# Matmuls without readers in TensorE's pauses: one decoder layer of cross attention and a quantised feed-forward block

## The chip, the cores and the metric

The kernel runs on one core of one Trainium2 chip. Its time is the device time of one execution in microseconds (us); a comparison takes the median of several executions. TensorE (PE) multiplies matrices, VectorE (DVE), ScalarE (ACT) and GpSimd (POOL) do the elementwise work, SyncE (SP) issues nearly all of the transfers. TensorE's clock is granted at one of two levels, 1.2 GHz (0.50 in the profile's rows) and 2.4 GHz (1.00).

## The reference

```python
x = x + cross_attention(layernorm(x), ctx)     # x 16 x 100 x 512, ctx 16 x 361 x 256, fp32
#   q = h @ Wq, k = ctx @ Wk, v = ctx @ Wv; 16 heads of 128; q and k through an RMS norm per head with gains
#   softmax(q k' / sqrt(128)) v, all heads joined, @ Wo
x = x + h_bitlinear(silu(gate) * up, w_down)   # gate, up = h_bitlinear(layernorm(x), w_gate / w_up)
#   h_bitlinear: Walsh-Hadamard rotation of the row, rounding to 8 bits by the row's largest value,
#   product with weights rounded to -1, 0, 1; 512 -> 2048 -> 512
```

## The kernel before

The kernel has three stages, each a block of its own: all engines finish one before any begins the next. An engine runs its instructions in the order written. An fp32 product is built from three fp32r matmuls (high by high, low by high, high by low), whose high and low parts ACT and DVE make.

**Queries** (`queries`). The 1600 tokens go in four groups of four sequences. For a group, DVE normalises the tokens (`xn`), TensorE transposes them into `psX` (`transposes`, L284), ACT and DVE split them into `xT_hi` and `xT_lo`, and for each of the 16 heads TensorE does 12 matmuls of 400 columns into `psQ` (L323), which ACT drains twice (`q_out`, stored to DRAM by SP, and the squares `sq`). `squares` (L295) sums the squares of four heads, DVE adds a constant (`ms`), and `factors` (L304) transposes the sums. Ahead of the first group Wq is fetched in pieces of 1 MB into a staging area of two halves. A piece may land in its half only when the piece before has been split, and ACT splits piece 2 only behind its drains of heads 0 and 1. The order on TensorE is: wait for the identity (`d_id`) and three of POOL's constants (`g_const`), transposes of group 0, the groups, and after the last group `squares` and `factors`.

**Attention** (`attention`). TensorE makes keys for a head (L732, 6 matmuls of 362 columns), and a product for head m waits until DVE has finished `k_lo` of head m - 2. After five heads `squares` (L744) sums the first four heads' squares; DVE, SP, POOL and a transfer turn them into the row factors `rk`, on which the first softmax waits. The later part is a pipeline of 64 units.

**Feed-forward** (`feed_forward`). 13 tiles of 128 tokens. `out_proj(t)` (L1296) is the output projection of tile t, 48 matmuls of 512 columns into `psA`. For tile 0 it stands ahead of the steps; its first half uses weights made in the stage before (`wo_first`), its second half weights that this stage fetches, splits on ACT and DVE, and counts in `v_w`. Then the chain for a tile is: residual and layer norm (DVE, with a power on POOL, L1224), `norm_T` (4 transposes, L1304), the split on ACT and DVE, `rotate_in` (8 matmuls of 256 columns, L1318), the row's scale and rounding, `q1_T` (L1327), `gate_up` (4 blocks of 8 matmuls of 512 columns, L1343), silu on ACT, product and rotation by DVE and POOL, `hidden_T` (transposes, L1355), `rotate_hidden` (L1365), rounding, a transposing transfer `turn_q2` by SP, and `down` (16 matmuls of 512 columns, L1375). `step(i)` holds work of up to four tiles (i to i + 3) in the order written, so that in the middle of the stage one tile's chain is hidden behind another tile's matmuls. Steps -2 and -1 fill this pipeline and steps 11 and 12 (`TILES - 2`, `TILES - 1`) empty it; from step 10 on no output projection is left. `high_o` and DVE's `o_lo` split the tile's input `o_in` (fetched by SP, L1160), and in step -2 DVE does this between the statistics and the norm of tile 0.

Of the kernel before, what the change touches and what calls it, by code (L numbers as in the profile page):

```python
# [22 lines left out]
P = 128  # L23
# [25 lines left out]
TILES = -(-T // TT)  # L49
# [72 lines left out]
def queries(nc, sbt, sem, passed, weights, ident, rq_all, neg_half, asums, d_q, x, wq, wk, wv, gq, gk, w_ff, ctxT,  # L122
# [7 lines left out]
    with ExitStack() as ctx:  # L130
# [25 lines left out]
        g_const, g_rstd, g_rq = s("g1_const"), s("g1_rstd"), s("g1_rq")  # L156
# [84 lines left out]
        @block.gpsimd  # L241
        def _(pool):
            nc.gpsimd.memset(neg_half[:], -0.5).then_inc(g_const, 1)
            nc.gpsimd.memset(sel[:], 0.0).then_inc(g_const, 1)
            pool.wait_ge(g_const, 2)
            nc.gpsimd.memset(sel[:, QW32 - 1:QW32], 1.0).then_inc(g_const, 1)
            nc.gpsimd.memset(weights["ones"][:], 1.0)
            for part in (cT_hi, cT_lo):
                nc.gpsimd.memset(part[:, :, :, SK:SKP].bitcast(F32), 0.0)

            def norm(g):
                pool.wait_ge(v_ve, g + 1)
                nc.gpsimd.tensor_tensor(rstd[:], ve[:], neg_half[0:SQ, :].to_broadcast([SQ, GB]),
                                        op=ALU.pow).then_inc(g_rstd, 1)

            def rms(g, part):
                pool.wait_ge(v_rq, g + 1)
                query_factors(nc, rq_all, neg_half, g, part).then_inc(g_rq, 1)

            def group(g, first, last):  # L260
                for h in range(H):
                    if h == 5 and not last:
                        norm(g + 1)
                    if 6 <= h < 14 and not first:
                        rms(g - 1, h - 6)

            norm(0)
            group(0, True, False)
            with pool.Fori(1, G - 1) as g:
                group(g, False, False)  # L270
            group(G - 1, False, True)

        @block.tensor
        def _(pe):
            pe.wait_ge(d_id, 16)
            pe.wait_ge(g_const, 3)

            def transposes(g):
                if due(g * DC):
                    pe.wait_ge(v_xlo, g * DC)  # L280
                for b in range(GB):
                    pe.wait_ge(v_xn, g * GB + b + 1)
                    for c in range(DC):
                        last = nc.tensor.transpose(psX[c][:, b * SQ:(b + 1) * SQ], xn[:, b, c * P:(c + 1) * P], ident[0:SQ, 0:SQ])  # L284
                    last.then_inc(p_xT, 1)

            def squares(g, k):

                pe.wait_ge(a_q, g * H + k * HG + HG)
                if k == 0:  # L290
                    if due(g):
                        pe.wait_ge(v_ms, g)
                for j in range(HG):
                    rows = slice(j * QW32, (j + 1) * QW32)
                    last = nc.tensor.matmul(psS[rows, 0:GT], sel[:, QW32 - 1 - k:2 * QW32 - 1 - k], sq[:, k % 2, j, :],  # L295
                                            start=(k == 0), stop=(k == NG - 1), tile_position=(0, j * QW32))
                last.then_inc(p_ss, 1)

            def factors(g):
                pe.wait_ge(v_ms, g + 1)  # L300
                pe.wait_ge(v_rq, g)
                apart(pe, pe_passed)
                for b in range(GB):
                    last = nc.tensor.transpose(psR[0:SQ, b, :], ms[:, b * SQ:(b + 1) * SQ], ident[:])  # L304
                last.then_inc(p_rq, 1)

            def group(g, first, last_group):
                for h in range(H):
                    if first and h == 0:
                        pe.wait_ge(v_first, 1)  # L310
                    elif first and h % HG == 0:
                        pe.wait_ge(used[h // HG % 2], h // HG // 2 + 1)
                    if first and h == 2:
                        pe.wait_ge(used[0], 1)
                    if due(g * H + h - 1):
                        pe.wait_ge(a_q, g * H + h - 1)
                    n = 0
                    for c in range(DC):
                        if h == 0:
                            pe.wait_ge(v_xlo, g * DC + c + 1)  # L320
                            apart(pe, pe_passed)
                        for w, m in ((wq_hi, xT_hi), (wq_hi, xT_lo), (wq_lo, xT_hi)):
                            last = nc.tensor.matmul(psQ[h % 2][:, 0:GT], w[:, c, h * D:(h + 1) * D], m[:, c, :],  # L323
                                                    start=(n == 0), stop=(n == 3 * DC - 1))
                            n += 1
                        if h == H - 1 and c < DC - 1:
                            last.then_inc(p_read, 1)
                    last.then_inc(p_q, 1)
                    if h % HG == 1 and h > HG:
                        squares(g, h // HG - 1)  # L330
                    elif h == 1 and not first:
                        squares(g - 1, NG - 1)
                    if h == 4 and not first:
                        factors(g - 1)
                    if h == 10 and not last_group:
                        transposes(g + 1)

            transposes(0)
            group(0, True, False)
            with pe.Fori(1, G - 1) as g:  # L340
                group(g, False, False)
            group(G - 1, False, True)
            squares(G - 1, NG - 1)
            factors(G - 1)

        @block.scalar
# [724 lines left out]
def feed_forward(nc, sbt, sem, passed, ident, neg_half, w127, o_in, d_stored, d_first, x, wo, d_wo, wo_first, had_in, o_dram,  # L1071
# [10 lines left out]
    with ExitStack() as ctx:  # L1082
# [56 lines left out]
        def real(t):  # L1139

            return not isinstance(t, int) or 0 <= t < TILES
# [138 lines left out]
        def _(pe):  # L1280
            def out_proj(t, heads):
                if heads[0] == 0:
                    if not (isinstance(t, int) and t == 0):
                        pe.wait_ge(v_o, NO + 1)
                    if due(t - 1):
                        pe.wait_ge(g_o, t - 1)
                    if due(t):
                        pe.wait_ge(v_xT, t)
                for h in heads:
                    if isinstance(t, int) and t == 0 and h % 2 == 0:  # L1290
                        pe.wait_ge(v_o, h // OH + 1)
                        if h >= HALF:
                            pe.wait_ge(v_w, (h - HALF) // 2 + 1)
                    hi, lo = (a[:, h, :] if h < HALF else b[:, h - HALF, :] for a, b in zip(wo_first, (wo_hi, wo_lo)))
                    for i, (w, m) in enumerate(((o_hi, hi), (o_hi, lo), (o_lo, hi))):
                        last = nc.tensor.matmul(psA[:], w[:, h, :], m, start=(h == 0 and i == 0),  # L1296
                                                stop=(h == H - 1 and i == 2))
                if heads[-1] == H - 1:
                    last.then_inc(p_out, 1)
# [69 lines left out]
            def down(t, k, rotated):  # L1369
# [7 lines left out]
                if k == 1:  # L1377
                    last.then_inc(p_down, 1)

            def step(i):  # L1380
                front = i + 2 if not isinstance(i, int) else min(i + 2, TILES)
                for j in range(NB):
                    if real(i + 1):
                        gate_up(i + 1, j)
                if real(i + 2):
                    out_proj(i + 2, range(AHEAD, H))
                if real(i + 1):
                    hidden_T(i + 1, 0)
                    hidden_T(i + 1, 1)
                if real(i):  # L1390
                    down(i, 0, front)
                    down(i, 1, front)
                if real(i + 1):
                    rotate_hidden(i + 1, 0)
                    hidden_T(i + 1, 2)
                    rotate_hidden(i + 1, 1)
                    hidden_T(i + 1, 3)
                if real(i + 2):
                    norm_T(i + 2)
                if real(i + 1):  # L1400
                    rotate_hidden(i + 1, 2)
                    rotate_hidden(i + 1, 3)
                if real(i + 2):
                    rotate_in(i + 2)
                if real(i + 3):
                    out_proj(i + 3, range(0, 4))
                if real(i + 2):
                    q1_T(i + 2)
                if real(i + 3):
                    out_proj(i + 3, range(4, AHEAD))  # L1410

            pe.wait_ge(v_ident, 1)
            out_proj(0, range(0, AHEAD))
            pipeline(pe, step, 3)
# [311 lines left out]
```

## Time and profile before

| | |
|---|---|
| median of 3 runs | 1480.15 us (1478.39 to 1481.29) |
| the profiled execution's own time | 1479.02 us |
| its span, first to last instruction | 1477.2 us |
| mean granted TensorE clock | 0.985 |
| TensorE busy | 1408.9 us, 95% of the span |
| VectorE, ScalarE, GpSimd busy | 65%, 64%, 35% |
| queries, attention, feed-forward | to 188 us, to 1050 us, to the end |

Busy is the time in which an engine had an instruction under way. A busy TensorE says nothing of its clock: at 1.2 GHz the same matmul is busy for longer. The idle time before an instruction, and what ended it, stand in square brackets at the end of its row.

### The profile page before, as it was taken

Reading aid. Unit: us, or ns where it says so; the run is one execution under the profiler, and the core shown is the slowest. Engines: PE = TensorE matmul, PEld = TensorE weight load, DVE = VectorE, ACT = ScalarE, POOL = GpSimd, SP = SyncE. Lnnn points to the kernel's source line nnn. Section 1 sums busy time; section 2 is a strip of 40 time slices with the busy share of each in tenths; the row PEclk is TensorE's granted clock in tenths of the full one; section 3 lists DMA queues with packets and bytes.
Section 4 is the critical chain, followed back from the end, with each engine's and each line's share of the span. In section 5 each row is a group of like instructions: output and inputs, shape, how many; then the busy total and the mean of one; then the engine's idle time right before and its main releaser. Section 6 shows DMA issues by size and latency. Waiting matters only on the chain. (4 is left out here: it accounts for less than half of the span.)

```text
span 1477.2 us, 30157 instructions
## 1 busy us (share of the span) xinstructions
PE 1408.9 (95%) x8818; PEld 1207.3 (82%) x8818; DVE 953.3 (65%) x2464; ACT 946.8 (64%) x2069; POOL 522.1 (35%) x323
## 2 busy tenths in 40 slices
PE   6999989999999999999999999998789999999995
PEld 6888868999999999999999999998566777677752
DVE  5312056677777777777777777766466777677764
ACT  4556658878888888788888788877324343434431
POOL 0033324433332223322333322335244555455533
PEclk9999999999999999999999999999899999999998
DMA  7767723343444443344434444334623223322211
GB/s 240 215 177 192 206 73 85 103 111 106 119 122 112 120 125 100 109 126 128 106 115 117 113 118 128 100 92 133 202 56 88 57 64 85 78 57 64 64 36 29
DMA packets 187782, 165.05 MB, mean 112 GB/s; under 512 B 111040, under 2 KB 162256, under 8 KB 185872
## 3 DMA queue, kind: packets, MB, share of 16 engines
q1 hardware_dynamic: 180752, 151.21, 37.5%
q10 hardware_dynamic: 6912, 12.59, 2.6%
q8 instruction: 35, 0.57, 0.2%
q14 instruction: 83, 0.68, 0.1%
HBM read 123.44 MB, written 33.14 MB: 106 GB/s over the span
## 5 line engine op out<-in xcount | busy, mean ns | idle before, releaser
L698 POOL TENSOR_TENSOR rk_sp<-ms_sp,neg_half 76x10 f32<-76x10 f32 (+1 forms) x128 | 242.2, 1908 | 596.0 <-DMA ms_sp<-ms 596.0
L1021 DVE CUSTOM_DVE_ANT_0 sc<-psS,rk 100x361 f32<-100x361 f32 x256 | 136.3, 532 | 108.1 <-PE psS L756 82.8
L873 ACT ACTIVATE pr<-ex,ri 100x361 f32<-100x361 f32 x256 | 152.9, 597 | 79.6 <-DVE ri L1010 79.4
L866 ACT ACTIVATE ex<-sc,nb,rq 100x361 f32<-100x361 f32 x256 | 175.2, 685 | 9.7 <-DVE nb L1028 9.5
L732 PE MATMUL psK<-cT_hi,wk_hi 128*128 128x362 f32 x512 | 171.1, 334 | 1.1 <-DVE k_lo L991 1.1
L854 ACT ACTIVATE k_hi<-psK 128x362 fp32r<-128x362 f32 x256 | 120.6, 471 | 78.3 <-PE psK L732 77.4
L732 PE MATMUL psK<-cT_lo,wk_hi 128*128 128x362 f32 x512 | 168.7, 330 | 0.0
L732 PE MATMUL psK<-cT_hi,wk_lo 128*128 128x362 f32 x512 | 168.6, 329 | 0.0
L991 DVE TENSOR_TENSOR k_lo<-psK,k_hi 128x362 fp32r<-128x362 f32 x256 | 134.5, 525 | 8.6 <-ACT sq L860 7.3
L781 PE MATMUL psZ<-pT_hi,cK_hi 120*128 120x400 f32 (+1 forms) x384 | 132.8, 346 | 0.0
L781 PE MATMUL psZ<-pT_hi,cK_lo 120*128 120x400 f32 (+1 forms) x384 | 132.3, 345 | 0.0
L781 PE MATMUL psZ<-pT_lo,cK_hi 120*128 120x400 f32 (+1 forms) x384 | 132.3, 345 | 0.0
L794 PE MATMUL psNV<-z,wv_sb 128*128 128x100 f32 x1024 | 124.9, 275 | 1.4 <-issue 1.4
L794 PEld LDWEIGHTS psNV<-z,wv_sb 128*128 128x128 f32 x1024 | 119.4, 192 | 2.0 <-issue 2.0
L769 PEld LDWEIGHTS psP<-ident,pr 100*120 100x120 f32 (+1 forms) x768 | 79.8, 165 | 48.0 <-issue 27.7
L860 ACT ACTIVATE sq<-psK 128x362 f32<-128x362 f32 x256 | 118.5, 463 | 0.0
L769 PE MATMUL psP<-ident,pr 100*120 100x100 f32 (+1 forms) x768 | 96.9, 262 | 7.1 <-ACT pr L873 6.9
L732 PEld LDWEIGHTS psK<-cT_hi,wk_hi 128*128 128x128 f32 x512 | 97.3, 190 | 5.6 <-DVE k_lo L991 4.4
L1002 DVE TENSOR_TENSOR pT_lo<-psP,pT_hi 121x600 fp32r<-121x600 f32 x128 | 99.0, 774 | 4.2 <-ACT pT_hi L881 3.0
L323 PE MATMUL psQ<-xT_hi,wq_hi 128*128 128x400 f32 x256 | 92.1, 360 | 6.1 <-ACT sq L397 3.0
L732 PEld LDWEIGHTS psK<-cT_lo,wk_hi 128*128 128x128 f32 x512 | 97.8, 191 | 0.0
L732 PEld LDWEIGHTS psK<-cT_hi,wk_lo 128*128 128x128 f32 x512 | 97.3, 190 | 0.0
(169 smaller groups left out, 3416.5 us busy)
## 6 DMA issues: line engine op xcount, KB each, us to landing
rk<-rk_dram SPq DMA_DIRECT2D x64, 564.1 KB
o_in<-o_dram SPq DMA_DIRECT2D x13, 1024.0 KB, 6.0
q_dram<-q_out SPq DMA_DIRECT2D x64, 200.0 KB, 4.4
q_in<-q_dram SPq DMA_DIRECT2D x64, 200.0 KB, 4.9
o_dram<-o SPq DMA_DIRECT2D x64, 200.0 KB, 5.4
stage<-in_w_ff SPq DMA_DIRECT2D x12, 1024.0 KB, 6.3
w_in<-in_w_ff ACTq DMA_DIRECT2D x48, 256.0 KB, 3.0
cT_in<-in_ctxT SPq DMA_DIRECT2D x16, 361.0 KB, 5.1
```

The costliest lines, as they stand in the source:

```text
L698: nc.gpsimd.tensor_tensor(rk_sp[:, cols], ms_sp[:, cols], neg_half[0:HG * SKR, :].to_broadcast([HG * SKR, n]), op=ALU.pow).then_inc(g_rk, 1)
L732: last = nc.tensor.matmul(psK[h % 2][:, 0:SKP], w[:, c, col:col + D], x[:, slot, c, :], start=(n == 0), stop=(n == 3 * CC - 1))
L769: last = nc.tensor.transpose(psP[0:KW[i], k, i * SQ:(i + 1) * SQ], pr[:, 2 * half + k, KO[i]:KO[i] + KW[i]], ident[0:SQ, 0:SQ])
L781: last = nc.tensor.matmul(psZ[c][:, 0:UQ], w[0:KW[i], slot, i, c * P:(c + 1) * P], x[0:KW[i], j % 2, i, :], start=(n == 0), stop=(n == 8))
L794: last = nc.tensor.matmul(psNV[:, h * SQ:(h + 1) * SQ], wv_sb[:, c, col:col + D], z[:, j % 2, c, h * SQ:(h + 1) * SQ], start=(c == 0), sto ...
L854: nc.scalar.activation(k_hi[:, j, h, :], psK[h % 2][:, 0:SKP], ACT.Copy)
L860: nc.scalar.activation(sq[:, j % 2, h, :], psK[h % 2][:, 0:SKP], ACT.Square).then_inc(a_k, 1)
L866: nc.scalar.activation(ex[:, h % 2, :], sc[:, h % 2, :], ACT.Exp, bias=nb[:, h % 2:h % 2 + 1], scale=rq[:, j % 2, h:h + 1], accum_out=rs[: ...
L873: nc.scalar.activation(pr[:, h, :], ex[:, h % 2, :], ACT.Copy, scale=ri[:, h % 2:h % 2 + 1]).then_inc(a_pr, 1)
L991: nc.vector.tensor_tensor(k_lo[:, j, h, :], psK[h % 2][:, 0:SKP], k_hi[:, j, h, :].bitcast(F32), ALU.subtract).then_inc(v_klo, 1)
L1002: nc.vector.tensor_tensor(two_heads(pT_lo, j, half), psP[0:KW[0], :, 0:3 * SQ].rearrange("p k (i q) -> p k i q", q=SQ), two_heads(pT_hi, j ...
L1021: nc.vector.tensor_tensor_reduce(out=sc[:, h % 2, :], in0=psS[0:SQ, 0:SK], in1=rk[:, j % 2, h, :], scale=1.0, scalar=-3.0e38, op0=ALU.mult ...
```

## The change

Two helpers, both called `busy`, issue matmuls with `start=True, stop=True` into a PSUM bank whose content nobody reads before the next real product overwrites it. No engine waits for them, and they wait for nothing of their own but what stands ahead of them on TensorE. The wait for POOL's constants becomes one for a fourth constant (`ones`) and comes ahead of the wait for the identity.

| place | matmuls | columns, type |
|---|---|---|
| ahead of the first transposes | 22 | 128, fp32 |
| after the first transposes | 11 | 128, fp32 |
| after the last head, ahead of `squares` | 4 | 400, fp32r |
| after it, ahead of `factors` | 6 | 400, fp32r |
| ahead of the first output projection | 6 | 512, fp32r |
| step -2, ahead of and after `norm_T(0)` | 27 and 5 | 512, fp32r |
| step 10, ahead of `q1_T(12)` | 11 | 512, fp32r |
| step 11, ahead of `hidden_T(12, 0)` | 27 | 512, fp32r |
| step 12, ahead of `down(12, 0)` | 27 | 512, fp32r |

```diff
-            nc.gpsimd.memset(weights["ones"][:], 1.0)
+            nc.gpsimd.memset(weights["ones"][:], 1.0).then_inc(g_const, 1)
...
+            def busy(bank, w, m, count):
+                for _ in range(count):
+                    nc.tensor.matmul(bank[:, 0:m.shape[-1]], w, m, start=True, stop=True)
+
+            pe.wait_ge(g_const, 4)
+            busy(psQ[0], weights["ones"][:], weights["ones"][:], 22)
             pe.wait_ge(d_id, 16)
-            pe.wait_ge(g_const, 3)
...
             transposes(0)
+            busy(psQ[0], weights["ones"][:], weights["ones"][:], 11)
             group(0, True, False)
...
             group(G - 1, False, True)
+            busy(psX[0], wq_hi[:, 0, 0:P], xT_hi[:, 0, :], 4)
             squares(G - 1, NG - 1)
+            busy(psX[0], wq_hi[:, 0, 0:P], xT_hi[:, 0, :], 6)
             factors(G - 1)
...
+            def busy(bank, count):
+                for _ in range(count):
+                    nc.tensor.matmul(bank[:], wo_first[0][:, 0, 0:P], wo_first[0][:, 0, :], start=True, stop=True)
...
                     out_proj(i + 2, range(AHEAD, H))
+                if isinstance(i, int) and i == TILES - 2:
+                    busy(psA, 27)
                 if real(i + 1):
                     hidden_T(i + 1, 0)
                     hidden_T(i + 1, 1)
+                if isinstance(i, int) and i == TILES - 1:
+                    busy(psA, 27)
                 if real(i):
                     down(i, 0, front)
...
                     hidden_T(i + 1, 3)
+                if isinstance(i, int) and i == -2:
+                    busy(psT[0], 27)
                 if real(i + 2):
                     norm_T(i + 2)
+                if isinstance(i, int) and i == -2:
+                    busy(psT[0], 5)
...
                     out_proj(i + 3, range(0, 4))
+                if isinstance(i, int) and i == TILES - 3:
+                    busy(psA, 11)
                 if real(i + 2):
                     q1_T(i + 2)
...
+            busy(psT[0], 6)
             pe.wait_ge(v_ident, 1)
             out_proj(0, range(0, AHEAD))
```

## Rows read from the trace of the kernel before

**Rows 1.** The page, part 2: granted clock in tenths, 40 slices of 37 us.

```profile
PEclk9999999999999999999999999999899999999998
```

**Rows 2.** Windows: length, busy (instructions) of PE, PEld, DVE, ACT, POOL; granted clock, DMA, GB/s.

```profile
187.40:194.20 6.80, 6.21 (x22) 5.66 (x21) 2.77 (x12) 1.67 (x4) 0.00 (x0) 0.50 0.26 84
...
1051.00:1057.80 6.80, 6.16 (x15) 4.83 (x16) 3.93 (x7) 3.60 (x6) 0.39 (x1) 0.50 0.90 310
...
1068.00:1078.10 10.10, 4.25 (x15) 3.58 (x16) 5.55 (x8) 0.60 (x1) 3.61 (x3) 0.50 0.79 244
...
1429.80:1436.60 6.80, 5.19 (x15) 2.00 (x16) 2.33 (x7) 3.68 (x5) 0.00 (x0) 0.50 0.40 77
```

**Rows 3.** Timeline, PE, feed-forward: start, duration, instruction, idle before it and its releaser.

```profile
1072.44 1.11 PE L1304 MATMUL psA<-ident,xr 128*128 128x128 f32 x4 [6.76 <-DVE xr L1567]
...
1430.63 0.61 PE L1327 MATMUL psT<-ident_b,q 128*128 128x128 bf16 x4 [2.76 <-DVE q L1611]
1432.02 9.48 PE L1343 MATMUL psB<-wt,q1T 128*128 128x512 fp8e4 x32 [0.78 <-ACT q1T L1456]
1448.10 1.97 PE L1355 MATMUL psT<-ident,stage 128*128 128x128 f32 x8 [6.60 <-DVE stage L1655]
...
1467.55 5.20 PE L1375 MATMUL psF<-wt,q2T 128*128 128x512 fp8e4 x16 [6.76 <-issue]
```

**Rows 4.** The chain that ended last, in order of time: start, us, what.

```profile
1051.64 14.05 PE psA L1296 x48
...
1074.97 2.07 PE psF L1318 x8
1077.04 3.38 PE psA L1296 x12
...
1124.30 0.87 PE psT L1355 x8
1125.17 3.45 PE psF L1375 x16
...
1134.04 0.96 PE psF L1318 x8
1135.00 2.76 PE psA L1296 x12
...
1403.23 7.06 PE psB L1343 x32
...
1450.07 5.32 PE psF L1375 x16
```

**Rows 5.** Timeline, PE, ACT and SP, first query group.

```profile
16.54 2.76 SPq L199 DMA_DIRECT2D stage<-in_wq  x2
...
19.51 0.54 PE L323 MATMUL psQ<-xT_lo,wq_hi 128*128 128x400 f32 x1
...
20.34 0.34 PE L323 MATMUL psQ<-xT_lo,wq_hi 128*128 128x400 f32 x1
...
22.32 1.92 ACT L354 ACTIVATE wq_hi<-stage 128x2048 fp32r<-128x2048 f32 x1
```

**Rows 6.** DMA issues, window 16 to 18 us: KB each, us from issue to landing.

```profile
stage<-in_wq SPq DMA_DIRECT2D x1, 1024.0 KB, 5.1
```

**Rows 7.** Timeline, PE, first keys of the attention.

```profile
188.88 0.65 PE L732 MATMUL psK<-cT_hi,wk_hi 128*128 128x362 f32 x1
...
197.24 0.81 PE L744 MATMUL psNV<-sq,sel 128*32 128x362 f32 x8
...
199.15 0.44 PE L732 MATMUL psK<-cT_hi,wk_hi 128*128 128x362 f32 x1
...
201.92 0.43 PE L732 MATMUL psK<-cT_hi,wk_hi 128*128 128x362 f32 x1
```

**Rows 8.** Timeline, SP, first load of `o_in` in the feed-forward.

```profile
1053.59 0.49 SPq L1160 DMA_DIRECT2D o_in<-o_dram  x1
```

**Rows 9.** DMA issues, window 1053.5 to 1054 us.

```profile
o_in<-o_dram SPq DMA_DIRECT2D x1, 1024.0 KB, 10.3
```

## The prediction, written before the changed kernel ran

> **What bounds the kernel now.** I read the page first. TensorE is busy for 95% of the span, so I looked for what it does at the half clock and where it stands still on the path to the end. The clock line of the page [rows 1] is nearly full everywhere and dips in the 29th slice and at the end; a slice is 37 us, so it hides stretches of a few us. Windows cut at the edges show them [rows 2]: the granted clock is 0.50 in 187.4 to 194.2, 1051.0 to 1057.8, 1068.0 to 1078.1 and 1429.8 to 1436.6. The reader is to see there that TensorE is busy for 6.2, 6.2, 4.3 and 5.2 us of these stretches, doing needed work at 1.2 GHz. The timeline and the chain show two more of the kind behind the pauses at the very end (below). In the first queries the clock record stands at full, but the durations tell another thing [rows 5]: the matmul at 19.51 takes 0.54 us and the same form at 20.34 takes 0.34. I take that stretch, from the first matmul at 14.0 to about 19.9, as cold too.
>
> Then the timeline of TensorE [rows 3] for what comes ahead of each cold stretch: pauses of 6.76, 2.76, 6.60 and 6.76 us, each ended by another engine or a transfer. The chain [rows 4] shows that the matmuls behind them are themselves on the path. Between 200 and 1040 us and from 1080 to 1428 us the clock is full, and the change touches nothing there.
>
> So the change is worth what the cold stretches cost on the path, if its matmuls hold the clock, and it costs what they overrun the pauses by.
>
> **What one added matmul costs.** Its form in the feed-forward, 512 columns of fp32r, is that of the output projection: 12 take 2.76 us warm [rows 4], 0.230 each. Cold, the windows row has 15 in 6.16 us [rows 2], 0.41 (0.43 from start to start, by the twofold clock). So 27 take 6.2 us warm against pauses of 6.76, 6.60 and 6.76; 11 take 2.5 against 2.76 [rows 3]. Each block ends 0.2 to 0.6 us before the real work is released, and nothing is queued behind it but that work. The 400-column ones at the end of the queries and the 128-column ones at the start lie ahead of waits too. The fp32 form with 128 columns does not occur before; its nearest relatives are transposes of 128 columns, 0.109 each warm (8 in 0.87) [rows 4], and I allow it from that to 0.43 (a cold 512-column one). 22 are then between 2.4 and 9.4 us behind a start near 1 us: at the upper end they would reach into the first transposes, whose result waits for the first piece of Wq anyway. I take them as hidden. The eleven behind the transposes take 1.2 to 4.7 us, in a pause of about two; I take 0, with up to 2.5 of loss if they run cold.
>
> **Start of the queries.** Warm, the stretch 14.0 to 19.9 would shrink by 0.34/0.54 or more, about 2.8 us. But TensorE is not what follows. ACT splits piece 2 of Wq at 22.32, without a wait, right after its drains of heads 0 and 1 [rows 5]. SP issued that piece at 16.54, when its half of the staging area came free, and it landed 5.1 us later, at 21.64 [rows 6]. Earlier drains leave ACT waiting for it, so the later splits, the next piece's load and the stores queued on SP behind it move by 22.32 - 21.64 = 0.7 us. Gain 0.7 (bounds -2.5 and +2.8).
>
> **End of the queries, start of the attention.** The added 4 and 6 matmuls of 400 columns stand before two waits. The 6.8 us of cold clock end at 194.2 [rows 2]; keys begin at 188.88 and the first `squares`, behind five heads, at 197.24 [rows 7]. Warm, a pair of heads takes 201.92 - 199.15 = 2.77 us, paced by the ACT and DVE work between product m - 2 and m. Five heads then end at 188.88 + 2 x 2.77 + 6 matmuls (6 x 0.18 = 1.1) = 195.5. `squares` starts 1.7 us earlier, and the chain behind it, through a transfer, POOL and a second transfer to the first softmax, moves with it. Gain 1.7 (bounds 0, if the chain is caught by something fixed, and 2.0).
>
> **First output projection.** 48 matmuls take 14.05 us [rows 4] and would take 48 x 0.230 = 11.0 warm, 3.0 less; the second half's weights arrive just in time for that, so 2.8. The six added ones take 1.4 us between the block's start at 1050.0 and the first real one at 1051.64. The stage boundary ahead of them stays idle. What is late next is `o_in` of tile 1: issued at 1053.59 [rows 8], landed 10.3 us later [rows 9], at 1063.9, while the projection ends at 1065.69 now. Its split stands on DVE ahead of tile 0's norm. So of 2.8 only 1065.69 - 1063.9 = 1.8 is sure; some slack between that split and the norm makes it 1.9.
>
> **Step -2.** The 27 cover the pause, the 5 cover the wait for the split. `norm_T` goes from 1.11 us to 4 x 0.109 = 0.44 (0.7 less), `rotate_in` from 2.07 to 0.96 (1.1 less), the twelve matmuls of `out_proj(1)` from 3.38 to 2.76, of which 0.5 counts since the rounding is then nearly as late [rows 3, 4]. Together 2.3; with the projection 4.2 (bounds 2.0 and 5.2).
>
> **Step 10.** `q1_T` is a little shorter, but ACT is rounding another tile when it ends, so nothing. `gate_up(12)` goes from 9.48 to 7.06 us for 32 [rows 3, 4]: 2.4 (bounds 1.2 and 2.6).
>
> **Step 11.** `hidden_T` of eight goes from 1.97 to 0.87, `down(11)` from 5.32 to 3.45 [rows 3, 4]: 1.1 + 1.9 = 3.0 (bounds 1.5 and 3.1).
>
> **Step 12.** `down(12)` goes from 5.20 to 3.45 [rows 3, 4]: 1.75 (bounds 1.0 and 1.8).
>
> The Trainium skill, page "TensorE: Matmul & The Clock Gate", section "Part 4: PE-mode transpose", says that transposes don't get the full clock and don't count as activity in the same way. The row differs in the first: eight transposes take 1.97 us behind a pause and 0.87 in the steady part [rows 3, 4]. By the page's rule the 0.7 and the 1.1 of transposes would fall out, and the sum below would be 12.0.
>
> **Sum.** 0.7 + 1.7 + 4.2 + 2.4 + 3.0 + 1.75 = 13.8 us. Against the profiled execution's own 1479.02 that is 1465.2; against the median of the runs, which is 1.1 higher, 1466.3. I say 1465.7.
>
> **Rivals.**
>
> One pause not held. Most likely at the first output projection, where TensorE still idles through the stage boundary (from 1048.5 to 1050.0) with only six matmuls behind it. The clock then falls during the projection, 1.9 us of gain go, and the step -2 gain stays, since 27 dense matmuls follow. 1467.6. For it: the clock fell before a pause of 2.76 us had ended [rows 2, 3], so short pauses suffice. Against it: the added matmuls are dense and fill the second half of this gap. Chance 0.15.
>
> The gains ahead of the attention are absorbed. Both the first group and the attention's first units hang on transfers. For it: rows 5 and 6. Against it: each transfer there is issued on the result of the work that moves. 0.7 + 1.7 go, 1468.1. Chance 0.08.
>
> The matmuls without readers don't move the clock, and fit in the pauses otherwise; the change then does nothing. 1480. Against it: in the row 1051.0 to 1057.8 [rows 2] just such matmuls bring the clock up. Chance 0.03.
>
> Slower: they overrun. The clock falls within the pause in spite of them, and the rest of a block runs at 0.43. If it falls 2.3 us in, 10 warm and 17 cold take 2.3 + 7.3 = 9.6 us where 6.7 are free; 2.9 late, three times (steps -2, 11, 12), with no gain anywhere: 1480 + 9 = 1489. The point from which it decides is a mean of 6.76 / 27 = 0.25 us for one. For it: the blocks are sized within 0.6 us of the pauses. Against it: 48 matmuls of the same form ran through 14 us and the clock rose in them and stayed. Chance 0.05.
>
> The forecast has the rest, 0.69. The Trainium skill, same page, section "Part 1: The HAM clock gate (the "warmup" mystery)", adds that the number of cold matmuls varies from run to run of one kernel. No run here shows it yet; by it single terms would come out 1 us either way in other runs, and the sum would stay.
>
> **Range and chances.** The high bounds of the terms together give 2.8 + 2.0 + 5.2 + 2.6 + 3.1 + 1.8 = 17.5, but the first will not reach its end with ACT waiting for the piece; with 0.7 there it is 15.4, and 1463.6 against the profiled time. With the spread of the runs the low end is 1462.3. On the other side one or two lost pauses and an absorbed start give 1470.5. 0.2% is 3 us, about what a measurement of this kernel tells from no change. All cases but the last two are faster by more: 0.92; same 0.03; slower 0.05.
>
> **What would show it.** In the changed kernel's profile: granted clock 1.00 from 187 to 194, 1051 to 1078 and 1430 to 1471; the 27 blocks in about 6.2 us; a piece-2 split on ACT that now waits for its transfer near 21.6; `squares` at about 195 less the 0.7 gained before; `out_proj(0)` in 11 to 11.3 us; `gate_up(12)` in 7.1; both `down` in 3.5. I am wrong if a block of 27 takes more than 6.7 us, if `hidden_T` or `down` waits for TensorE to finish it, or if the attention's 64 units take longer than before.

## The result and the profile after

| | before | changed |
|---|---|---|
| median, runs | 1479.27 us, 6 | 1468.95 us, 6 (1467.73 to 1471.92) |
| ratio | | 0.9933, 95% interval 0.992 to 0.9946 |
| profiled execution: own time, span | 1479.02, 1477.2 | 1468.72, 1466.8 |
| mean granted clock | 0.985 | 0.999 |

The kernel became 10 us faster (9.9 by the ratio, with an interval of 8 to 11.8); the forecast was 13.8. Below, cold means at the half clock and warm at the full one. First the clock line of the profile's page, in slices of 37 us:

```profile
PEclk9999999999999999999999999999999999999999
```

The dips of [rows 1] are gone. Windows over the stretches that were cold, the first four to be held against [rows 2] (length, busy of PE, PEld, DVE, ACT, POOL, granted clock, DMA, GB/s):

```profile
187.40:194.20 6.80, 5.31 (x30) 4.47 (x30) 3.34 (x13) 2.88 (x7) 0.00 (x0) 1.00 0.29 87
1050.30:1057.10 6.80, 6.32 (x27) 4.61 (x25) 3.25 (x6) 3.10 (x5) 0.38 (x1) 1.00 0.95 299
1066.00:1076.00 10.00, 8.86 (x45) 6.91 (x43) 6.33 (x11) 1.49 (x3) 3.05 (x3) 1.00 0.96 309
1426.00:1432.80 6.80, 5.68 (x29) 2.43 (x28) 3.16 (x8) 4.19 (x6) 0.00 (x0) 1.00 0.40 77
1441.90:1455.70 13.80, 13.59 (x82) 10.63 (x83) 6.82 (x15) 5.10 (x7) 4.70 (x4) 1.00 0.05 19
1451.70:1462.30 10.60, 9.96 (x45) 6.40 (x43) 2.83 (x8) 2.13 (x2) 0.00 (x0) 1.00 0.26 49
```

The last two, behind the pauses of steps 11 and 12, stand against these of the kernel before:

```profile
1446.90:1453.70 6.80, 5.60 (x17) 3.07 (x18) 2.53 (x3) 1.20 (x2) 3.35 (x1) 0.50 0.01 2
1464.00:1470.80 6.80, 3.25 (x8) 1.17 (x9) 0.85 (x2) 0.44 (x1) 0.00 (x0) 0.50 0.40 77
```

Granted clock 1.00 in each, where it was 0.50. The matmuls behind the pauses, from TensorE's timeline (start, duration, instruction, idle before it), against [rows 3]. L1392 is the added form of the feed-forward:

```profile
1063.18 6.28 PE L1392 MATMUL psT<-wk_hi 128*128 128x512 f32 x27
1070.35 0.66 PE L1313 MATMUL psA<-ident,xr 128*128 128x128 f32 x4 [0.88 <-DVE xr L1592]
...
1423.84 2.68 PE L1392 MATMUL psA<-wk_hi 128*128 128x512 f32 x11
1426.76 0.40 PE L1336 MATMUL psT<-ident_b,q 128*128 128x128 bf16 x4 [0.25 <-DVE q L1636]
1428.04 7.21 PE L1352 MATMUL psB<-wt,q1T 128*128 128x512 fp8e4 x32 [0.87 <-ACT q1T L1481]
1434.89 6.51 PE L1392 MATMUL psA<-wk_hi 128*128 128x512 f32 x27
1441.91 1.09 PE L1364 MATMUL psT<-ident,stage 128*128 128x128 f32 x8 [0.51 <-DVE stage L1680]
...
1451.72 6.33 PE L1392 MATMUL psA<-wk_hi 128*128 128x512 f32 x27
1458.66 3.61 PE L1384 MATMUL psF<-wt,q2T 128*128 128x512 fp8e4 x16 [0.61 <-issue]
```

The pauses of 6.76, 2.76, 6.60 and 6.76 us have shrunk to 0.88, 0.25, 0.51 and 0.61, and none of the released instructions shown stands behind an added one. `gate_up` went from 9.48 to 7.21 us, the eight transposes from 1.97 to 1.09, `down` from 5.20 to 3.61.

Milestones in the traces show where the 10.4 us of span were won. The first column is a start time. Each other one is the time between two events of one trace: the first key and the first `squares` of the attention; that `squares` and the feed-forward's first work on ACT; that work and the split of tile 1's `o_in` on ACT, the first `gate_up`, and the end of the span.

| trace | last `squares` of queries | first key to first `squares` | that to feed-forward | to `o_in` split | to `gate_up(0)` | feed-forward in all |
|---|---|---|---|---|---|---|
| before | 184.87 | 8.36 | 852.80 | 15.76 | 31.92 | 427.16 |
| changed | 185.19 | 6.69 | 853.80 | 14.97 | 28.60 | 417.49 |

From `gate_up(0)` to the end it is 395.24 against 388.89. So 6.35 us come from behind `gate_up(0)`, where only the last three steps have added matmuls, 3.3 from the start of the feed-forward, and 0.7 from the queries and the attention together (the stage begins at 1049.31 instead of 1050.04).

### The profile page after: what moved, and what is told of

Same layout as the page of the kernel before. It is cut to its first block and busy times, and to the rows that moved or that the text cites. A ratio compares the mean times of both kernels' runs of the same rounds, so it can differ in the third digit from the quotient of the medians.

```text
span 1466.8 us, 30515 instructions
## 1 busy us (share of the span) xinstructions
PE 1427.9 (97%) x8997; PEld 1225.7 (84%) x8997; DVE 954.2 (65%) x2464; ACT 947.1 (65%) x2069; POOL 524.0 (36%) x323
## 5 line engine op out<-in xcount | busy, mean ns | idle before, releaser
L1019 DVE RECIPROCAL ri<-rs 100x1 f32<-100x1 f32 x256 | 41.3, 161 | 86.0 <-ACT ex L875 74.7
L1454 ACT ACTIVATE hT_hi<-psT 128x512 fp32r<-128x512 f32 x52 | 29.7, 596 | 104.4 <-PE psT L1364 104.4
```

## The experiments

Twelve experiments in three groups of four, in the order of the table; those of one group ran on one chip and share its runs of the kernel before. `after_again` and `after_third` are the changed kernel itself, `no_start_2` and `ff_only_2` repeat two others. The milestones come from one profiled execution of each. All ratios are to the kernel before, with 95% intervals; the milestones are those of the table above.

| kernel | median us | ratio | last `squares` | key to `squares` | attention | `o_in` split | `gate_up(0)` | feed-forward |
|---|---|---|---|---|---|---|---|---|
| after_again | 1469.09 | 0.9943 (0.993 to 0.9955) | 186.88 | 6.71 | 852.99 | 14.77 | 28.48 | 417.19 |
| ff_only | 1468.51 | 0.9943 (0.9929 to 0.9957) | 184.28 | 7.47 | 854.54 | 13.31 | 27.01 | 415.58 |
| queries_only | 1477.38 | 0.9998 (0.9986 to 1.001) | 187.42 | 6.71 | 854.51 | 14.84 | 31.52 | 427.03 |
| no_start | 1466.7 | 0.9926 (0.9913 to 0.9938) | 185.42 | 6.68 | 855.06 | 14.15 | 27.86 | 416.61 |
| forty | 1475.28 | 0.9983 (0.9973 to 0.9993) | 187.22 | 6.71 | 854.27 | 14.82 | 30.32 | 423.57 |
| thirteen | 1475.06 | 0.998 (0.9968 to 0.9991) | 187.23 | 6.71 | 853.85 | 14.52 | 29.22 | 422.48 |
| turning | 1467.24 | 0.9929 (0.9913 to 0.9946) | 184.85 | 6.70 | 852.95 | 14.98 | 28.71 | 417.57 |
| no_boundary | 1469.15 | 0.9941 (0.9925 to 0.9958) | 186.41 | 6.69 | 853.99 | 14.64 | 28.36 | 417.17 |
| lean | 1469.75 | 0.9923 (0.9909 to 0.9936) | 187.69 | 6.70 | 854.50 | 14.47 | 28.69 | 417.38 |
| no_start_2 | 1468.41 | 0.9922 (0.9908 to 0.9935) | 186.85 | 6.70 | 853.54 | 14.27 | 28.49 | 417.18 |
| ff_only_2 | 1470.29 | 0.9929 (0.9915 to 0.9943) | 187.11 | 7.56 | 854.71 | 13.99 | 27.64 | 416.48 |
| after_third | 1469.76 | 0.993 (0.9917 to 0.9944) | 185.51 | 6.69 | 853.49 | 14.91 | 28.55 | 417.27 |

The theory tested (theory A in the first group) is that the gain is that of the clock in the feed-forward, and that the query stage's share does not reach the end.

**after_again**, the changed kernel once more.

> The changed kernel once more, as the measure for the other three on this chip. In its trace the feed-forward stage (from its first instruction at 1049.3 to the end) was 9.7 us shorter than before and everything ahead of it only 0.7. Both theories expect 10 us less than the kernel before (1468 to 1471 against 1478 to 1481), the feed-forward stage within 0.5 us of the first trace, and the start of that stage anywhere from 1047 to 1052, since the attention in between has its own spread. If that start lies within 0.3 us of 1049.3 again, the 0.7 is a property of the kernel and not of one execution.

The feed-forward took 417.19 against 417.49. Its start came at 1050.21, 0.9 later than in the first trace: the 0.7 us won ahead of the stage there are not a property of the kernel.

**ff_only**

```diff
-            busy(psQ[0], weights["ones"][:], weights["ones"][:], 22)
...
-            busy(psQ[0], weights["ones"][:], weights["ones"][:], 11)
...
-            busy(psX[0], wq_hi[:, 0, 0:P], xT_hi[:, 0, :], 4)
...
-            busy(psX[0], wq_hi[:, 0, 0:P], xT_hi[:, 0, :], 6)
```

> Leaves out the 22, 11, 4 and 6 matmuls of the query stage; those of the feed-forward stay. Theory A (the held clock pays only where it shortens the path, and the query stage's 0.7 and 1.7 us were absorbed by transfers and the attention's pipeline): 0 to 1 us slower than the changed kernel, feed-forward stage as in it, its start near 1050. Theory B (the query stage's gain of 2.4 is real and the first trace had an unlucky attention): 2 to 2.5 us slower than the changed kernel, start of the feed-forward 2 us later than there.

The same ratio as the changed kernel on that chip, 0.9943: theory A, as far as intervals of 0.0013 can say. The added matmuls of the feed-forward alone carry the gain. In this trace the stage was even 1.6 to 1.9 us shorter than in those of the changed kernel: the load of `o_in` landed 9.9 us after its issue instead of 11.3 to 11.5, and the split came 1.5 to 1.7 us earlier.

**queries_only**, the other half: the calls of `busy` in the feed-forward are taken out.

```diff
-                    busy(psA, 27)
...
-                    busy(psT[0], 27)
...
-            busy(psT[0], 6)
```

(all six places of the feed-forward likewise)

> Leaves out all added matmuls of the feed-forward and keeps the 43 of the query stage. Theory A: 0 to 1 us faster than the kernel before, not to be told from it; the first squares of the attention at 195.5 as in the changed kernel, start of the feed-forward 0 to 1 us earlier than before. Theory B: 2 to 2.5 us faster than before. Both expect the four cold stretches of the feed-forward back, at the lengths of the kernel before (14.05 us for the first projection, 9.5 for gate_up of the last tile, 5.3 and 5.2 for the last two down products), and so a difference of this kernel to the changed one of 9 to 10 us.

Ratio 0.9998, with an interval that leaves 2.1 us of gain barely in: theory A again. The feed-forward took 427.03 us, as before (427.16); the first projection, though cold in part, took 12.75 and not the expected 14.05. The end of the stage, from the timeline of TensorE, has the pauses and the slow products of [rows 3] back:

```profile
1450.48 1.97 PE L1364 MATMUL psT<-ident,stage 128*128 128x128 f32 x8 [6.60 <-DVE stage L1669]
...
1468.61 6.17 PE L1384 MATMUL psF<-wt,q2T 128*128 128x512 fp8e4 x16 [6.81 <-issue]
```

**no_start**: only the 22 and 11 are out.

```diff
-            busy(psQ[0], weights["ones"][:], weights["ones"][:], 22)
...
-            busy(psQ[0], weights["ones"][:], weights["ones"][:], 11)
```

> Leaves out the 22 and 11 matmuls at the start alone. Theory A: the stage's loads decide the first group, so head 12 and the end of the queries come within 0.4 us of the changed kernel's times, earlier or later; the total is the same within 0.5 us. Theory B: 0.7 us slower, and ACT splits piece 2 of Wq without a wait near 22.3 again. The first squares of the attention should lie 1.7 us earlier than in the kernel before by both, since the 4 and 6 matmuls at the stage's end are still there.

The first `squares` came 6.68 us behind the first key, as expected of both. ACT split piece 2 at 22.82 without a wait, and the last `squares` of the queries came at 185.42, between the changed kernel's 185.19 and 186.88. The median was even 2.4 us lower than the changed kernel's on this chip, which neither theory had; the third group looks at that. The trace is of the slowest of the six executions (1469.18) and can't show where the others were faster.

**forty**: the three blocks of 27 become 40.

```diff
-                    busy(psA, 27)
+                    busy(psA, 40)
```

> The three blocks of 27 (steps -2, 11 and 12) are 40 long. In the changed kernel 27 took 6.2 us, 0.229 each, and ended 0.88, 0.51 and 0.61 us before the real work was released. Theory A (one costs 0.229 us at the held clock and is free only while the pause lasts): each block overruns by 13 x 0.229 less its slack, 2.1 + 2.5 + 2.4 = 7.0 us slower than the changed kernel, 1475 to 1477. Rival (the real work does not queue behind the block one for one, for instance because part of it is hidden by the engine's queue): under 3 us slower.

The median, 1475.28, is in the expected range. The feed-forward took 423.57 us, 6.1 to 6.4 more than in the three traces of the changed kernel; the rival had under 3. In the timeline a block now runs straight into the real work, which has lost its idle time:

```profile
1439.14 9.43 PE L1392 MATMUL psA<-wk_hi 128*128 128x512 f32 x40
1448.41 1.03 PE L1364 MATMUL psT<-ident,stage 128*128 128x128 f32 x8
```

13 more matmuls at a slack (the idle time left behind a block) of 0.5 to 0.9 us cost 6.1 to 6.4 us in three places, 7.0 were expected; what is beyond the pause is paid nearly one for one.

**thirteen**: the same blocks are 13 long.

```diff
-                    busy(psA, 27)
+                    busy(psA, 13)
```

> The same three blocks are 13 long: 3.0 us of work, then 3.5 to 3.8 us of standing still. Theory A (the clock must be held up to the end of the pause; before, it fell 2 to 5 us into a pause): it falls in most of the three, and the cold work behind is back: up to 2.3, 3.0 and 1.75 us, together 3 to 7 us slower than the changed kernel, with 0.50 in the windows behind these pauses. Rival (some activity within the pause is enough): as the changed kernel within 1 us, clock 1.00 behind all three.

The feed-forward took 422.48 us, 5.0 to 5.3 more than in the changed kernel's traces, and the median, 1475.06, lies 5.9 and 7.8 us above those of the two kernels on the same chip that hold the clock in the three pauses (`no_boundary`, `turning`). Windows over the rest of a pause and the work behind it, steps 11 and 12:

```profile
1441.20:1444.80 3.60, 0.00 (x0) 0.00 (x0) 3.52 (x5) 0.00 (x0) 1.57 (x2) 0.97 0.00 0
1444.80:1450.00 5.20, 5.16 (x21) 3.19 (x22) 1.38 (x2) 1.19 (x2) 2.20 (x1) 0.69 0.01 3
1459.20:1463.10 3.90, 0.08 (x1) 0.02 (x1) 1.17 (x2) 0.76 (x1) 0.00 (x0) 0.81 0.56 108
1463.10:1468.00 4.90, 4.89 (x12) 1.73 (x13) 0.00 (x0) 0.00 (x0) 0.00 (x0) 0.50 0.11 21
```

and the two pieces of work themselves:

```profile
1444.84 1.97 PE L1364 MATMUL psT<-ident,stage 128*128 128x128 f32 x8 [3.68 <-DVE stage L1680]
...
1463.11 6.25 PE L1384 MATMUL psF<-wt,q2T 128*128 128x512 fp8e4 x16 [3.83 <-issue]
```

Standing still for 3.7 or 3.8 us after 13 matmuls was enough for the clock to fall, and the eight transposes take 1.97 us again as in [rows 3], `down` 6.25. In step -2 TensorE stood still for 4.05 us, `norm_T` still ran warm (0.68 us), and the clock fell right behind it: the five added matmuls took 2.40 us instead of 1.40, and `gate_up(0)` came 0.6 to 0.7 us later. The block has to reach the end of the pause.

**turning**: 56 transposes of the identity instead of 27 matmuls.

```diff
+            def turning(bank, count):
+                for _ in range(count):
+                    nc.tensor.transpose(bank[:, 0:P], ident[:], ident[:])
...
-                    busy(psA, 27)
+                    turning(psA, 56)
```

> The same three blocks are 56 fp32 transposes of the identity (0.109 us each warm, 6.1 us) instead of 27 matmuls of 512 columns. Theory A (what counts is that TensorE is busy): clock 1.00 through the pauses, total within 1 us of the changed kernel. Rival, which the Trainium skill, page TensorE: Matmul & The Clock Gate, section Part 4: PE-mode transpose, gives (transposes do not count as activity): the clock falls in the block as it did in the empty pause, the rest of the transposes takes 0.25 us each, as the eight behind the pause did before, a block takes about 10 us and overruns by 3.5, and the cold work behind is back: 3 x 3.5 + 7 = 17 us slower than the changed kernel.

```profile
1434.09 6.28 PE L1397 MATMUL psA<-ident 128*128 128x128 f32 x56
1440.88 1.09 PE L1364 MATMUL psT<-ident,stage 128*128 128x128 f32 x8 [0.52 <-DVE stage L1685]
```

The block took 6.28 us, 0.112 each, and the work behind it was warm. The windows over block and successor:

```profile
1434.10:1440.90 6.80, 6.28 (x58) 6.05 (x56) 6.61 (x8) 0.69 (x1) 4.70 (x4) 1.00 0.00 1
1440.90:1446.00 5.10, 5.10 (x31) 3.29 (x32) 1.29 (x2) 1.62 (x3) 2.14 (x1) 1.00 0.01 3
```

The clock is 1.00 in both. Transposes hold it as well as matmuls do: the feed-forward took 417.57 us, and the ratio is 0.9929 beside the changed kernel's 0.993 to 0.9943. The Trainium skill, page "TensorE: Matmul & The Clock Gate", section "Part 4: PE-mode transpose", says that the full clock doesn't engage for transposes and that they don't count as busy time in the same way. These ran at 0.112 us each with the clock at 1.00 and kept it there, so its rule does not hold for them. Whether transposes would also raise the clock from the half, no run shows.

**no_boundary**

```diff
-            busy(psT[0], 6)
             pe.wait_ge(v_ident, 1)
```

> Leaves out the six matmuls ahead of the first output projection alone. Theory A: the clock falls near the start of the projection again and its 48 matmuls take 14 us instead of 12.4; since the load of o_in decides what follows, 1 to 1.6 us slower than the changed kernel, and the step -2 block, being dense, brings the clock back by its end. Rival (the 6 do nothing; the two traces so far hold 6 that took 1.6 us and 6 that took 2.65 us, so the clock can fall all the same): no difference, the projection 12.4 to 12.8 us.

The rival. The projection took 12.76 us, and nothing changes: ratio 0.9941 beside the changed kernel's 0.993 to 0.9943, and `gate_up(0)` 28.36 us behind the stage's start beside 28.48 to 28.60. In `after_again` the six are there and took 2.65 us, and the window shows a partly cold projection all the same:

```profile
1050.20:1057.00 6.80, 6.77 (x23) 5.49 (x24) 4.37 (x6) 4.31 (x6) 1.37 (x1) 0.75 0.96 288
```

Its `gate_up(0)` came no later for it (28.48). What decides in these is a transfer, in `no_boundary` too, where the split waited for a load of 11.2 us. ACT in the changed kernel (timeline), and the load of `o_in` (DMA issues: KB, us to landing):

```profile
1064.28 1.92 ACT L1447 ACTIVATE o_hi<-o_in 128x2048 fp32r<-128x2048 f32 x1 [2.45 <-DMA o_in<-o_dram]
```

```profile
o_in<-o_dram SPq DMA_DIRECT2D x1, 1024.0 KB, 11.3
```

That is not so in every execution. In `no_start_2`, where the six took 2.80 us, and in `lean`, which has none, the load took 10.1 and 10.3 us, and the split waited for the projection. ACT in `no_start_2`:

```profile
1064.99 1.92 ACT L1445 ACTIVATE o_hi<-o_in 128x2048 fp32r<-128x2048 f32 x1 [3.27 <-PE psA L1303]
```

Their `gate_up(0)` came at 28.49 and 28.69. In `ff_only`, with as early a load (9.9) and a projection that was warm throughout (11.14 us), it came at 27.01. With a warm projection their splits could have begun when the loads landed, 13.5 and 13.8 us into the stage, and from the split to `gate_up(0)` the changed kernel needs 13.6 to 13.7 us. So the six could pay some 1.2 us when the load is early (an estimate from these traces), and nothing when it is late.

**lean, no_start_2, ff_only_2, after_third**, side by side on one chip. `lean` leaves out the 22, 11 and 6:

```diff
-            busy(psQ[0], weights["ones"][:], weights["ones"][:], 22)
...
-            busy(psQ[0], weights["ones"][:], weights["ones"][:], 11)
...
-            busy(psT[0], 6)
```

> Leaves out what has shown no gain: the 22 and 11 at the start and the six at the stage boundary; keeps 4 and 6 at the end of the queries and all later ones. Theory A (the start blocks cost the first group up to 1.6 us through the order of its transfers: the last squares of the queries came at 186.5 on average in seven traces with them, at 184.9 in three without; the six pay nothing because the load of o_in decides the stage's first 15 us): 1.5 to 2.5 us faster than the changed kernel, last squares of the queries at 184.3 to 185.5, first gate_up 28.4 us after the stage's start. Rival (these differences are spread between executions): the same as the changed kernel within 0.5 us.

> The kernel without the 22 and 11 at the start, again. Theory A: 1.5 to 2.5 us faster than the changed kernel on this chip too, as it was before (1466.7 against 1469.1), and within 0.5 us of the kernel that also lacks the six. Rival: the same as the changed kernel within 0.5 us.

> Only the added matmuls of the feed-forward, again. If the 4 and 6 at the end of the queries are worth the 1.7 us of their step, it is 1.5 to 2 us slower than the kernel that lacks the start blocks alone (1468.5 against 1466.7 before); if the attention's pipeline absorbs them, the same within 0.5 us.

> The changed kernel a third time, as the measure for the other three on this chip: 1468 to 1470, last squares of the queries at 185 to 187.5.

The idea that the start blocks cost time did not hold. `lean` had its last query `squares` at 187.69, later than any trace with the blocks; the mean over eight traces with them is 186.3 and over six without 186.0, in a spread of 184.3 to 187.7. `lean` and `after_third` have equal medians (1469.75 and 1469.76). `no_start` was 2.4 and 1.3 us below the changed kernel in the two groups, with ratios of 0.9926 and 0.9922 against 0.9943 and 0.993; on the first chip five of its six executions lie below all six of the changed kernel, on the second they mix, and the intervals overlap, so that it beats the changed kernel is likely at most and not shown, and no trace gives a cause. `ff_only` lay 1.8 and 1.9 us above `no_start` on both chips, the size of what the 4 and 6 save in the keys, with intervals that overlap too.

## Why the prediction was right or wrong

The time, 1468.95, lies in the range of 1462.3 to 1470.5, 3.2 us above the point. The mechanism is the one that was forecast, and the experiments show it for the feed-forward; the terms ahead of it did not arrive in the total, and the others were mostly too large. The measured time lies nearer to two of the rivals than to the point: gains ahead of the attention absorbed (1468.1, chance 0.08), and one pause not held (1467.6, chance 0.15). Parts of both happened, as told below.

**One matmul, and the fit in the pauses: right.** 27 are busy for 6.28, 6.51 and 6.33 us in the rows above, forecast 6.2, with 6.7 as the sign of being wrong; the slacks are 0.25 to 0.88, forecast 0.2 to 0.6. `forty` confirms the price, `thirteen` that the whole pause must be covered. The slower rival, decided by 0.25 us for one, is excluded at 0.23. The 22 fp32 matmuls at the start took 8.03 us, within their bounds of 2.4 to 9.4, and ended ahead of the first transposes. The eleven took 2.64 us (bounds 1.2 to 4.7), and the first real product stands right behind them without a wait, as `factors` does behind the six at the stage's end; what these overran by no row shows.

**Start of the queries, 0.7: it did not arrive.** The step itself came out to the tenth: ACT's split now waits for piece 2, in the timeline of ACT in the changed kernel:

```profile
21.52 1.91 ACT L363 ACTIVATE wq_hi<-stage 128x2048 fp32r<-128x2048 f32 x1 [1.98 <-DMA stage<-in_wq]
```

It is 0.8 us earlier than in [rows 5]. What failed is the sentence that the later splits, loads and stores move with it. ACT then waited 1.05 us for piece 3 and 4.6 us for two stores, and the transposes of group 1 began at 43.75 against 43.88. Over 14 traces the end of the stage shows no effect of the start blocks.

**Attention's start, 1.7: right there, not resolved in the total.** First key to first `squares` fell from 8.36 to 6.69 us, 1.67, and to 6.68 to 6.71 in ten other traces with the 4 and 6. Without them two more traces have 7.47 and 7.56: the keys are not equally cold in every execution, and 8.36 was the long case. The attention behind it takes 852.8 to 855.1 us with a mean of 853.9 in the eleven traces with them and 854.0 in the three without, so it does not give the time back, but its spread and that of the queries are larger than the term. (In the profiled pair it was 1.0 us longer than before, 853.80 against 852.80, which the prediction names as a sign of being wrong; the other traces put that down to the spread.) `queries_only` shows no gain within 2 us, `ff_only` beside `no_start` shows 1.8 twice; how much of the 1.7 counts stays open.

**First output projection, 1.9: mis-sized, 0.8, and even that is not shown to be the clock's.** The step named the right successor, the load of `o_in`, and gave it the landing time of before, 10.3 us [rows 9]. In the changed kernel it took 11.3, and the split began 14.97 us into the stage against 15.76. That load lies between other loads in a saturated stretch (DMA share 0.95). The projection itself was to take 11 to 11.3 us; it took 12.42, though warm, with 0.78 us of waiting for the second half's weights in one place. And the 14.05 us that the gain was counted from were a long case: with nothing added ahead of it the cold projection took 12.75 in `queries_only` and `lean` and 12.76 in `no_boundary`. `queries_only`, without any added matmul in this stage, had the split at 14.84, and `no_boundary` at 14.64; so the 0.8 belongs to the spread. The rival "one pause not held" did happen there, in three of the ten traces that have the six: `after_again`, `turning` and `no_start_2`. It cost nothing in the first two, where the load was late.

**Step -2, 2.3: about right.** From the start of `norm_T` to `gate_up(0)` it went from 9.52 us to 7.56, 2.0 (3.0 beside `queries_only`, cold there as well, with 10.54). Of that 0.46 lies ahead of `rotate_in`, forecast 0.7, and 1.5 behind, forecast 1.6. Counted from the `o_in` split it is 16.16 to 13.63, 2.5; but the 0.6 more lies ahead of `norm_T`, where TensorE does nothing on the path. `lean` and `no_start_2`, whose split waited for the projection as it did before, need the 6.66 us from split to `norm_T` that the kernel before needed (6.64).

**Step 10, 2.4; step 11, 3.0; step 12, 1.75: right, each 0.2 to 0.3 too large.** Measured from start to start: `gate_up(12)` to `hidden_T` 16.08 to 13.87, 2.2; `hidden_T` to `down(12)` 19.45 to 16.75, 2.7; `down(12)` to the end 9.65 to 8.14, 1.5. I priced the cold work by its duration and the warm by rows within a dense stream; behind even a short pause the warm eight transposes take 1.09 and not 0.87, and `down` 3.6 and not 3.45.

Together 11.35 us were forecast for the feed-forward and 9.7 to 10.0 came (from 427.16 to between 417.19 and 417.49), and of 2.4 ahead of it 0.7 in the profiled pair, which is within the spread of that part. The prediction's remark that single terms would come out about 1 us either way in other executions is borne out by the keys and by the cold projection: each of these two terms was counted from the row of one trace that was a long case.

## What to carry to other kernels

Where the matmuls behind a wait of TensorE run at the half clock (here behind waits of 2.76 to 6.76 us) and are on the path, fill the wait up to its end with matmuls (or transposes) that nobody reads. Size them by the warm duration: those beyond the pause are paid nearly in full, and a pause left open behind them loses the clock again (here 3.7 to 4.1 us). Look first at what is late next: where a transfer decides, a warm TensorE only waits for it longer. Price each term from the start behind one pause to the start behind the next, take the cold duration from more than one trace, and don't sum gains smaller than the spread of the stage that they lie in.

## What the hardware showed that was not expected

Transposes of 128 columns hold the clock through 6.3 us as matmuls of 512 columns do, and themselves run at 0.112 us warm against 0.25 cold.

The stretch of cold keys at the attention's start varied between executions of kernels without help there, by 0.9 us (8.36 and 7.47 to 7.56), and the cold first projection by 1.3 (14.05 and 12.75).

The clock doesn't fall at one point of a pause. In the kernel before it had fallen within one of 2.76 us; in `thirteen` it stood through 4.05 us and fell behind `norm_T`. At the stage boundary TensorE stood still for 1.56 us ahead of the six added matmuls, which took 1.60 to 1.63 us in seven traces and 2.65, 2.73 and 2.80 in three. In those three the clock fell while the six ran; in all four traces without the six a part of the projection ran cold.

22 fp32 matmuls of 128 columns appear as 44 records and took 8.03 us, 0.37 each, where eleven behind the transposes took 2.64, 0.24 each; so part of the first 22 ran cold.
